# Attention: two units' products with the values one block later, and the work between them one block earlier

## What is computed

```python
x_proj = x @ Wqkv + bqkv
q = x_proj[:, :, :C].reshape(B, n_head, T, hd)
k = x_proj[:, :, C:2 * C].reshape(B, n_head, T, hd)
v = x_proj[:, :, 2 * C:].reshape(B, n_head, T, hd)
att = jnp.einsum('bhtd,bhsd->bhts', q, k) * (1.0 / jnp.sqrt(jnp.float32(hd)))
causal = jnp.tril(jnp.ones((T, T), dtype=bool))
att = jnp.where(causal, att, jnp.float32(-jnp.inf))
att = jax.nn.softmax(att, axis=-1)
y = att @ v
y = jnp.transpose(y, (0, 2, 1, 3)).reshape(B, T, C)
return y @ Wproj + bproj
```

## Time and profile before

| | us |
|---|---|
| median of 3 runs | 3762.44 |
| lowest, highest | 3750.83, 3772.56 |
| profiled execution, its own time | 3763.16 |
| its span, first to last instruction | 3761.3 |
| attention layer with its start and end | 1081 to 3135 |
| in it: TensorE, VectorE, ScalarE, GpSimd busy | 2003.12, 1745.44, 1432.38, 1158.09 |
| mean granted TensorE clock (of full speed) | 0.978 |

### The profile page before, as it was taken

How to read it: one execution, slowest core, us unless ns; L and a number is a source line. 1 busy time by engine, 2 the same in 40 slices (tenths; PEclk the granted TensorE clock), 3 DMA queues, 4 the chain that set the end, 5 groups by cost and what they waited for, 6 DMA issues and landing times. The chain is left out here.

```text
span 3761.3 us, 76026 instructions
## 1 busy us (share of the span) xinstructions
PE 3560.0 (95%) x25550; PEld 2347.9 (62%) x25550; DVE 2952.9 (79%) x9275; ACT 2183.7 (58%) x4151; POOL 1666.4 (44%) x2027
## 2 busy tenths in 40 slices
PE   6999899999689999999999999999999998999997
PEld 5888666666455665566656656655666555666664
DVE  8998666766688888888888888888888893676775
ACT  1110456655337766766676667667667665656654
POOL 2332123223345556656555565565565511223323
PEclk9999899999879999999999999999999999999999
DMA  2333112111497978787887879788887832121211
GB/s 74 100 98 109 57 46 68 54 59 35 116 140 111 126 115 129 120 127 123 122 127 119 132 116 126 116 119 123 124 134 121 120 41 80 40 68 46 68 46 45
DMA packets 694291, 361.16 MB, mean 96 GB/s; under 512 B 297905, under 2 KB 660913, under 8 KB 693937
## 3 DMA queue, kind: packets, MB, share of 16 engines
q1 hardware_dynamic: 693936, 356.62, 53.5%
HBM read 204.49 MB, written 150.99 MB: 95 GB/s over the span
## 5 line engine op out<-in xcount | busy, mean ns | idle before, releaser
L1862 ACT ACTIVATE att_probs<-att_s 128x512 f32<-128x512 f32 x2304 | 1212.5, 601 | 461.2 <-PE att_s L2001 234.4
L1737 DVE CUSTOM_DVE_ANT_0 att_s<-att_s,att_above 128x384 f32<-128x384 f32 (+3 forms) x2048 | 950.2, 519 | 132.8 <-PE att_s L1981 127.1
L1981 PE MATMUL att_s<-att_ks,att_qs 48*128 48x512 f32 (+3 forms) x3072 | 896.0, 401 | 5.7 <-DVE att_maxima L1740 3.6
L2001 PE MATMUL att_s<-att_qs,att_ks 49*128 49x512 f32 (+3 forms) x3072 | 852.4, 373 | 20.5 <-DVE att_maxima L1737 5.2
L2001 PEld LDWEIGHTS att_s<-att_qs,att_ks 49*128 49x128 f32 x3072 | 487.6, 186 | 464.0 <-ACT att_probs L1862 271.6
L1740 DVE TENSOR_REDUCE att_maxima<-att_s 128x1 f32<-128x512 f32 x1024 | 661.9, 684 | 98.3 <-PE att_s L1981 93.2
L2029 PE MATMUL att_o_ps<-att_probs,att_vs 128*32 128x512 f32 (+3 forms) x6144 | 620.5, 497 | 25.1 <-ACT att_probs L1862 22.1
L1981 PEld LDWEIGHTS att_s<-att_ks,att_qs 48*128 48x128 f32 x3072 | 485.9, 189 | 26.4 <-DVE att_maxima L1737 8.9
L1097 PE MATMUL ffn_h2p<-ffn_h,ffn_w 128*128 128x512 f32 x768 | 365.0, 598 | 3.0 <-ACT ffn_h L968 0.9
L1951 PE MATMUL att_s<-att_mask,att_places 64*128 64x128 bf16 (+1 forms) x2560 | 327.7, 212 | 0.0
L1737 DVE DVE_READ_ACCUMULATOR2_ANT att_maxima<- 128x1 f32 x2048 | 293.0, 143 | 0.0
(11 more groups left out here) (292 smaller groups left out, 6384.8 us busy)
## 6 DMA issues: line engine op xcount, KB each, us to landing
att_staged<-qk_scratch SPq DMA_DIRECT2D x768, 128.0 KB, 7.6
qk_scratch<-att_parts SPq DMA_DIRECT2D x128, 512.0 KB, 3.4
ffn_x<-x SPq DMA_DIRECT2D x64, 512.0 KB, 5.2
ssm_x<-in_L_attn_a_x_dram SPq DMA_DIRECT2D x32, 512.0 KB, 3.7
x<-ssm_y SPq DMA_DIRECT2D x32, 512.0 KB, 3.0
x<-ffn_y SPq DMA_DIRECT2D x32, 512.0 KB, 2.9
att_x<-x SPq DMA_DIRECT2D x32, 512.0 KB, 7.4
v_scratch<-att_v_tok SPq DMA_DIRECT2D x32, 512.0 KB, 5.3
```

The source lines that it names most:

```text
L1737: last = v.tensor_tensor_reduce(scores, scores, above[:, CH - w:CH], 1.0, -3.0e38, ALU.add, ALU.max, to)
L1862: a(probs[u % PROBS][2 * g + p][:, 0:n], bank[:, 0:n], ACT.Exp).then_inc(exp_done, 1)
L1981: last = mm(bank[:, col:col + w], rows_of(qs[buf], g, KROWS, p, BT * blk, BT * (blk + 1)), rows_of(ks[buf], g, KROWS, p, t0, t1), start=k ...
L2001: last = mm(bank[:, col:col + w], rows_of(ks[buf], g, SHIFT + 1, p, BT * j, BT * (j + 1)), rows_of(qs[buf], g, SHIFT + 1, p, t0, t1), star ...
```

## The change

Two tables of positions change; no instruction is added or removed.

```diff
-    TIMES_V_SLOTS = {2: 0, 3: 1, 4: 2, 5: 3, 7: 4, 8: 5, 10: 6, 11: 7}
+    TIMES_V_SLOTS = {2: 0, 3: 1, 4: 2, 6: 3, 7: 4, 9: 5, 10: 6, 11: 7}
...
-        finish = [] if first else {0: [(3, "turn", 0), (6, "out", 0), (7, "turn", 1), (9, "out", 1), (10, "turn", 2)],
-                                   1: [(1, "out", 2), (2, "turn", 3), (6, "out", 3)]}.get(q, [])
-        project = {0: [(1, 6), (4, 7)], 1: [(4, 0), (7, 1), (9, 2)], 2: [(1, 3), (4, 4), (6, 5), (9, 6)],
+        finish = [] if first else {0: [(3, "turn", 0), (5, "out", 0), (7, "turn", 1), (8, "out", 1), (10, "turn", 2)],
+                                   1: [(1, "out", 2), (2, "turn", 3), (5, "out", 3)]}.get(q, [])
+        project = {0: [(1, 6), (4, 7)], 1: [(4, 0), (7, 1), (8, 2)], 2: [(1, 3), (4, 4), (5, 5), (8, 6)],
                    3: [(1, 7)]}[q] if more else []
-        project += [(2, 0), (4, 1), (6, 2), (8, 3), (9, 4), (11, 5)] if q == 3 and more2 else []
+        project += [(2, 0), (4, 1), (5, 2), (7, 3), (8, 4), (11, 5)] if q == 3 and more2 else []
```

## The result

| | us |
|---|---|
| changed kernel, median of 20 runs (lowest, highest) | 3779.52 (3765.55, 3795.25) |
| kernel before, 20 runs beside it | 3764.92 (3750.83, 3779.21) |
| ratio, 95% interval | 1.0038, 1.0028 to 1.0048 |
| profiled execution, span | 3774.1 |
| mean granted TensorE clock of the runs | 0.972, before 0.977 |

0.38% slower, 14.3 us (10.5 to 18.1): within the 0.5% that counts as no change, in the range, and 13.5 us above the forecast of 3766. The waits came and went about as forecast. What was not in the sum is TensorE's clock, which falls to half behind some of the new waits.

A forecast was written before the change was run, and what follows sets the result against it. TensorE was taken to bound the attention layer, so only waits move: -0.31, +0.51, -0.77 and +0.92 us in q0 to q3, 15, 15, 15 and 14 times, give +4.3 us on 3763.16, forecast 3766 us (chance 0.60), range 3745 to 3794.

The forecast's parts named there:

- (a): Block 5: the wait before the fourth unit's products goes, 0.44 us in q3 and q1, 0.40 in q0 and q2.
- (b): Block 9 of q0, q1, q2: the third scores pair's wait for VectorE's bank goes, 0.37 us each.
- (c): Block 8 of q2 and q3: the third pair's wait behind short block 7 goes, 0.28 and 0.38 us.
- (d): Block 7 of q1, q2, q3: third pair waits for an exponential held by the fourth unit's products, 0.28 us added.
- Rival 2: Block 7: the exponential does not hold up the third pair; -12.6 us, 3754 us; chance 0.09.
- (e): q0: VectorE's addition and moments before block 6's first maximum delay block 7's third pair, 0.46 us added.
- (f): q3 block 5: the first projection waits for GpSimd's split of the transposed activation, 1.46 us added.
- (g): q1 block 8: the projection waits for GpSimd's split of the transposed activation, 1.04 us added.
- a subtraction of trace times: How the new split waits in q3 block 5 and q1 block 8 were priced: 1.46 and 1.04 us.
- Rival 1: Splits are early enough, so no new waits on them in q3 and q1; -31.7 us, 3731 us; chance 0.09.
- Rival 3: Blocks 9 to 11 of q1 and q2: VectorE cannot follow three short blocks; 27 us, 3793 us; chance 0.09.
- Rival 4: VectorE, not TensorE, is the bound, so waits taken from TensorE come back; 3763 us; chance 0.05.

The follow-up runs named there:

- run 4: Changed kernel with the third unit's put-off piece multiplied early, alone at the end of block 5; 3764.9 us, ratio 1.0037 to the kernel before.
- run 3: Changed kernel, but q3 blocks 5 and 6 and q1 blocks 8 and 9 as before; 3718.2 us, ratio 0.9915 to the kernel before.
- run 10: Repeat: changed kernel, but q3 blocks 5 and 6 and q1 blocks 8 and 9 as before; 3716.3 us, ratio 0.9903 to the kernel before.
- run 7: Changed kernel with useless weight products filling TensorE's waits on the splits in q3 and q1; 3766.3 us, ratio 1.0008 to the kernel before.
- run 1: Changed kernel, but the old tables in the last batch entry; 3765.1 us, ratio 1.0033 to the kernel before.
- run 6: Changed kernel, but q1 blocks 8 and 9 as before; 3760.7 us, ratio 0.9994 to the kernel before.
- run 5: Changed kernel, but q3 blocks 5 and 6 as before; 3740.5 us, ratio 0.9940 to the kernel before.
- run 8: Kernel before with only the change's second half, blocks 7 to 9, in q0, q2 and q3; 3751.0 us, ratio 0.9994 to it.

## Why the prediction was right, and where not

**Which waits go and come.** (a): 22.3 us to 0.1. (b): in q0 blocks 8 and 9 took 5.26 and now 4.88, 0.38 less, forecast 0.37. (c) with (d) and (b) in q2: blocks 7 to 9 took 7.37 and now 7.01, 0.36 less, forecast 0.37. (d): 55 waits of ScalarE, and the third pair of block 7 stands 0.84 behind the block's start, which was 2003.97 in this q0, forecast 0.85:

```profile
2004.81 0.50 PE L2001 MATMUL att_s<-att_qs,att_ks 49*128 49x512 f32 x1
```

That the figure fits so well is in part luck: the exponential starts 0.19 to 0.20 into the block, not 0.11, and the pair 0.05 to 0.06 behind its end, not 0.14. Rival 2, that (d) doesn't bind, falls with that and the rows under run 4.

**(e)** was too dear. In that q0 the addition and the moments do stand before the first maximum, which starts 2002.60 - 2001.59 = 1.01 into block 6, beside the earlier trace rows, not 1.2:

```profile
2001.69 0.69 DVE L1770 TENSOR_TENSOR att_x_res<-att_x_ps,att_x_res 128x512 f32<-128x512 f32 x1
...
2002.60 1.26 DVE L1740 TENSOR_REDUCE att_maxima<-att_s 128x1 f32<-128x512 f32 x2
```

Block 7 of q0 grew by 0.32, as in q1 and q2, so the exponential bound it there too, and (e) cost nothing of its own. That is 0.14 to 0.18 x 15, 2 to 3 us of the sum; q1 came out 2.7 us dearer than its forecast, and q0 otherwise, q2 and q3 2.8 cheaper, which cancel, so that 4.3 became 2.2.

**(f) and (g)** were right as waits. q3: blocks 5 and 6 took 5.58 and take 6.61, +1.03; forecast 1.46 - 0.44 = 1.02. q1: blocks 8 and 9 +0.75, forecast 1.04 - 0.37 = 0.67; open idle in the timeline of TensorE:

```profile
2040.79 1.63 PE L2056 MATMUL att_x_ps<-att_xnT,att_wqkv 128*128 128x512 f32 x6 [1.10 <-POOL att_xnT L1552]
```

**The step that failed** is the price of those waits: "a subtraction of trace times". By its terms the two moves in question cost 1.30 x 14 in q3 and 0.67 x 15 in q1, 28 us, the gains that come with them taken off. By medians it is 33; measured it is 46 and 51 (runs 3 and 10).
**Rivals 1, 3 and 4.** Rival 1, the splits are early enough: wrong as a forecast (27 waits), and its -31.7 is near the -32 and -36 of runs 3 and 10 by luck, since in those the gains of (a) in q3 and of (b) in q1 are missing. Rival 3, three short blocks too dear for VectorE: blocks 9 to 11 of q1 and q2 take 2.05, 2.24 and 2.27, no wait. Rival 4, VectorE is the bound: with waits taken from TensorE the time fell by all of them in run 3, so it falls, though run 4 shows VectorE's bank holding TensorE up in single blocks.

**The sum.** By the prediction's terms the moves other than those two have -24 us, measured -32 and -36 (medians -31), and those two +28, measured +46 and +51. Both were off, one way and the other, and the whole stays within 0.5% of the kernel before, as forecast, in part by luck. Of the second error some 5 us are in the lengths of the blocks, and for the rest the runs show the half clock behind the waits (run 7: 11 us, some 6 either way). The sum of one profile, 2.2 by medians and 13 by the clock, comes close to the measured 14.3 only because it leaves out the 9 us that the profile of before lost in its own half-clock stretches; that this fits is luck.

## What to carry to other kernels

A new wait of TensorE is priced by its length and by what its clock does behind it; where TensorE is the bound and the new waits are as long as the 1.36 us here, give the second a term of its own. Before a sum of such losses is set against the measured difference, take off what the kernel before loses in the same way. When a reordering gains nothing, sum it by place: here two of eight moves ate the gain of the other six, and leaving those two (the first projection stays behind the block in which its split ends) gives a kernel 0.9% faster than the one before. Where such a wait can't be avoided, cheap products that need no new data can keep the clock up, as in run 7.

## What the runs showed of the hardware

- The same 1.36 us of idle, at the same point of fourteen q3s, was followed by 1.2 GHz in six in the profile of the changed kernel, in seven in those of runs 1 and 6, and in one in that of run 4; in the others the clock stayed at 2.4 GHz. With the idle filled it stayed there in all fourteen. What decides between them stays open.
- The 1.1 us of idle in block 8 of q1 were not followed by half clock in the profiles of the changed kernel and runs 1 and 5. In one q1 of each of the three the split was late and the idle lasted 3.32, 1.87 and 3.06 us, and 10 us at 1.2 GHz came behind it.
- Over the runs of one kernel the time follows the mean granted clock: the 20 runs of the changed kernel have clocks of 0.970 to 0.975 and times from 3795 down to 3766 us, and 0.001 of mean clock goes with 4.4 us (a straight line through the 20); over the runs of before beside the experiments it goes with 2.1 to 3.1. The mean clock of a set of runs told of the lost time where one profile did not (run 8).
- One profiled execution can stand 18 to 20 us from the median of its kernel, mostly through what lies outside the steady quads (run 8's first profile below it, run 5's above). Medians of repeated blocks were within 0.02 us between the three profiles of run 8's kernel: those are what to compare.
